# Query bias of a fused attention and mixture-of-experts layer carried by the query weights instead of by a matmul of its own

## The reference, cut to what matters

```python
xn = _layernorm(x)                                  # (x - mean) / sqrt(var + eps) over the 256 channels
q = (xn @ Wq + bq).reshape(b, h, t, dh)             # b=4, h=16, t=1024, dh=128
k = (xn @ Wk + bk).reshape(b, t, h, dh).transpose(0, 2, 3, 1)
v = (xn @ Wv + bv).reshape(b, t, h, dh).transpose(0, 2, 1, 3)
logits = einsum('bhtd,bhds->bhts', q, k) / sqrt(dh) # causal mask, softmax
out = einsum('bhts,bhsd->bhtd', softmax(logits + mask), v)
attn = out.transpose(0, 2, 1, 3).reshape(b, t, h * dh) @ Wo + bo
# moe: shared expert + top 6 of 64 experts, 128 slots each, on the same xn
x = x + attn + moe
```

## Time and profile before

| | |
|---|---|
| median of 3 runs | 1869.17 us (1868.74 to 1877.19) |
| the profiled execution | 1875.93 us |
| its span, first to last instruction | 1874.2 us, 49686 instructions |
| PE matmul busy | 1696.9 us (91%) |
| PE weight loads busy | 1312.7 us (70%) |
| DVE busy | 1402.9 us (75%) |
| ACT busy | 1081.9 us (58%) |
| POOL busy | 1116.8 us (60%) |
| bias matmuls L592 | 128, 49.7 us busy |
| granted PE clock, mean | 0.962 of full speed |

### The profile page before, as it was taken

How to read it: one execution, slowest core, us unless ns; L and a number is a source line. 1 busy time by engine, 2 the same in 40 slices (tenths; PEclk the granted TensorE clock), 3 DMA queues, 4 the chain that set the end, 5 groups by cost and what they waited for, 6 DMA issues and landing times. The chain is left out here.

```text
span 1874.2 us, 49686 instructions
## 1 busy us (share of the span) xinstructions
PE 1696.9 (91%) x19217; PEld 1312.7 (70%) x19217; DVE 1402.9 (75%) x3128; ACT 1081.9 (58%) x2347; POOL 1116.8 (60%) x1006
## 2 busy tenths in 40 slices
PE   3699999999999999999977789999998999999997
PEld 3477777776777777777756767777776777767775
DVE  8677777777677777777644458888888888888885
ACT  2566666666666666666622255665655655666554
POOL 1256666767767676676720047666666666666653
PEclk8799999999999999999977689999999999999998
DMA  9377767666656656557557657777778778877775
GB/s 372 104 152 130 128 108 133 125 121 109 115 87 101 102 98 95 100 97 125 99 120 217 181 103 137 124 128 127 151 131 143 126 144 133 134 125 125 151 119 110
DMA packets 686658, 245.04 MB, mean 131 GB/s; under 512 B 637456, under 2 KB 674721, under 8 KB 685536
## 3 DMA queue, kind: packets, MB, share of 16 engines
q1 hardware_dynamic: 657472, 197.83, 59.2%
q0 software_dynamic: 18432, 33.64, 7.1%
q10 hardware_dynamic: 10528, 10.49, 1.7%
HBM read 57.11 MB, written 50.46 MB: 57 GB/s over the span
## 5 line engine op out<-in xcount | busy, mean ns | idle before, releaser
L485 POOL TENSOR_TENSOR prob<-prob 128x128 f16<-128x128 f32 (+7 forms) x512 | 652.5, 1279 | 636.5 <-ACT prob L874 630.0
L867 ACT ACTIVATE prob<-prob,nmax 128x128 f32<-128x128 f32 (+7 forms) x512 | 396.8, 775 | 598.4 <-DVE prob L1312 552.3
L708 PE MATMUL ps_s<-kT,qT 128*128 128x512 f16 (+3 forms) x2304 | 460.0, 327 | 4.4 <-DVE prob L1312 4.3
L723 PE MATMUL ps_o<-probT,vh 128*128 128x256 f16 (+1 forms) x3840 | 427.4, 265 | 3.4 <-DMA probT<-prob 3.4
L1312 DVE TENSOR_SCALAR_CACHE_REDUCE prob<-ps_s,neg_scale 128x128 f32<-128x128 f32 (+7 forms) x512 | 412.1, 809 | 11.3 <-PE ps_s L710 7.4
L723 PEld LDWEIGHTS ps_o<-probT,vh 128*128 128x128 f16 x3840 | 368.3, 99 | 49.4 <-issue 5.2
L874 ACT CAST prob<-prob 128x128 f16<-128x128 f32 (+7 forms) x512 | 341.4, 667 | 2.6 <-DMA probT<-prob 0.3
L708 PEld LDWEIGHTS ps_s<-kT,qT 128*128 128x128 f16 x2304 | 201.5, 98 | 144.7 <-issue 4.5
L737 PE MATMUL ps_y<-wo,oT 128*128 128x256 f16 x1536 | 211.6, 274 | 58.1 <-DVE oT L1327 55.8
L1341 DVE SCALAR_TENSOR_TENSOR resid<-ps_y,yscale,resid 128x256 f32<-128x256 f32 x512 | 223.1, 477 | 15.0 <-PE ps_y L737 5.3
L525 POOL DMA_INDIRECT got<-expert_out,slot_idx x192 | 196.2, 1022 | 32.5 <-issue 28.5
(11 more groups left out here) (182 smaller groups left out, 1661.0 us busy)
## 6 DMA issues: line engine op xcount, KB each, us to landing
dispatched<-zeros SPq DMA_DIRECT2D x16, 512.0 KB, 14.3
probT<-prob SPq DMA_TRANSPOSE x512
ex<-dispatched SPq DMA_DIRECT2D x16, 512.0 KB, 4.5
expert_out<-eo ACTq DMA_DIRECT2D x16, 512.0 KB, 3.7
eup<-in_L_ffn_w_up_dram SPq DMA_DIRECT2D x64, 64.0 KB, 2.1
dispatched<-xn,slot_idx POOLq DMA_INDIRECT x192
xn_columns<-xnth SPq DMA_DIRECT2D x24, 128.0 KB
got<-expert_out,slot_idx POOLq DMA_INDIRECT x192
```

The costliest lines, as they stand in the source:

```text
L485: pool.tensor_tensor(low_cols(j), prob_cols(j).rearrange("p (r k) -> p r k", k=P), high_cols(j), ALU.subtract).then_inc(p_low, 1)
L708: pe.matmul(s_cols(j, lo, hi), qT[:, u, a, j * P:(j + 1) * P], kT[:, u, c, lo:hi], start=(n == 0), stop=(n == 2 and hi < w))
L723: mm = pe.matmul(ps_o[:, lo:2 * P], vh[:, u, a, r * D:(r + 1) * D], probT[:, PT_AT[c] + 2 * r + s, lo:], start=(r + n == 0), stop=(r == 2 ...
L867: nc.scalar.activation(prob_cols(j), prob_cols(j), ACT.Exp, bias=nmax[:, j:j + 1], scale=-1.0, accum_out=rsum[:, i % 2, j:j + 1]).then_inc ...
```

## The change

Since a normalised token sums to zero over its 256 channels, a constant row can be subtracted from all rows of `Wq` without changing the product. The change subtracts row 0 of `Wq` from every row, so that row 0 becomes zero and channel 0 of the tokens no longer counts; it then writes `bq` into row 0 and replaces channel 0 of the tokens by ones. The bias matmul goes. Because keys and values still need the true channel 0, the queries get a copy `xq` of the first 128 channels: partition 0 holds ones (high half) and zeros (low half), partitions 1 to 127 are copied from `xT` or from DRAM. The second 128 channels are still read from `xT`.

```diff
             sp.wait_ge(bias_zero, 1)
-            for n, b in enumerate((bq, bq, bk, bv)):
+            for n, b in ((0, bq), (2, bk), (3, bv)):
...
             for n in (0, 1, 3, 2):
                 sp.dma_start(stg[n].rearrange("p (k n) -> p k n", k=(KC, KC, KC, H)[n]), views[n]).then_inc(wload[n], 16)
+                if n == 0:
+                    sp.dma_start(wq_row0, Wq[0:1, :].rearrange("a n -> (a n)").partition_broadcast(P)).then_inc(row0_in, 16)
...
-            sp.dma_start(resid[:, TB:2 * TB, :], x_v[:, TB:2 * TB, :]).then_inc(x_in[1], 16)
             sp.wait_ge(xn0_ready, TB)
             sp.dma_start(xn_d, xn0[:]).then_inc(xn0_stored, 16)
+            sp.wait_ge(xt0_low, 4)
+            sp.dma_start(xq[1:P, :, :], xT[1:P, :, 0, :]).then_inc(xq_in, 16)
+            sp.wait_ge(wq_shifted, 1)
+            sp.dma_start(resid[:, TB:2 * TB, :], x_v[:, TB:2 * TB, :]).then_inc(x_in[1], 16)
             sp.wait_ge(const_ready, 1)
...
                 for n in range(2):
                     sp.dma_start(xT[:, n, :, 0:TPH], xnT_d[:, n, :, b * T:b * T + TPH]).then_inc(xT_head, 16)
+                sp.dma_start(xq[1:P, :, 0:TPH], xnT_d[1:P, :, 0, b * T:b * T + TPH]).then_inc(xT_head, 16)
                 for n in range(2):
                     sp.dma_start(xT[:, n, :, TPH:], xnT_d[:, n, :, b * T + TPH:(b + 1) * T]).then_inc(xT_in, 16)
+                sp.dma_start(xq[1:P, :, TPH:], xnT_d[1:P, :, 0, b * T + TPH:(b + 1) * T]).then_inc(xT_in, 16)
...
+            pool.memset(xq[0:1, 0, :], 1.0).then_inc(xq_ones, 1)
+            pool.memset(xq[0:1, 1, :], 0.0).then_inc(xq_ones, 1)
+            pool.wait_ge(wload[0], 16)
+            pool.wait_ge(row0_in, 16)
+            pool.wait_ge(wmax_step, 1)
+            w3 = stg[0].rearrange("p (k n) -> p k n", k=KC)
+            pool.tensor_tensor(w3, w3, wq_row0.unsqueeze(1).to_broadcast([P, KC, HD]), ALU.subtract).then_inc(wq_shifted, 1)
...
                 elif h == 0 and half == 0:
-                    pe.wait_ge(xT_head, 32 * (i // H))
+                    pe.wait_ge(xT_head, 48 * (i // H))
...
                 if i == 0 and half == 0:
-                    pe.wait_ge(bq_step, 3)
-                    pe.wait_ge(bias_taken, 2)
-                pe.matmul(ps_t[:, half, :].rearrange("p (m t) -> p m t", t=TPH), bq_rows[:],
-                          bq_pick[:, half * (H // 2):(half + 1) * (H // 2)].unsqueeze(2).to_broadcast([P, H // 2, TPH]),
-                          start=True, stop=False)
+                    pe.wait_ge(xq_in, 16)
+                    pe.wait_ge(xq_ones, 2)
...
-                                           xT[:, c, k, h * TPH:(h + 1) * TPH], start=False, stop=(n + k == 3 and m % (H // 2) == H // 2 - 1))
+                                           (xT[:, c, k] if k else xq[:, c])[:, h * TPH:(h + 1) * TPH], start=(n + k == 0), stop=(n + k == 3))
...
                 elif h == 0 and half == 0:
-                    pe.wait_ge(xT_in, 32 * (i // H))
+                    pe.wait_ge(xT_in, 48 * (i // H))
...
+            act.wait_ge(wq_shifted, 1)
+            act.dma_start(stg[0][0:1, 0:HD], bq.rearrange("(a n) -> a n", a=1)).then_inc(bq_in, 16)
             def high_weights(n):
                 act.wait_ge(wscale_step, 8 if n < 2 else 20)
+                if n == 0:
+                    act.wait_ge(bq_in, 16)
...
-                    dve.wait_ge(bq_step, 1)
-                    V.tensor_scalar(bq_rows[0:64, :], bias_rows[0:64, :], scales[0:64, 0:1], None, ALU.mult).then_inc(bq_step, 1)
-                    dve.wait_ge(bq_step, 2)
-                    V.scalar_tensor_tensor(bq_rows[32:64, :], bias_rows[32:64, :], scales[32:64, 0:1], bq_rows[32:64, :],
-                                           ALU.mult, ALU.subtract).then_inc(bq_step, 1)
...
-            V.tensor_tensor(bq_pick[:], ident[:, 0:H], ident[:, 32:32 + H], ALU.add).then_inc(bias_taken, 1)
```

More of the change, by code:

```diff
@@ L78, in causal_attention_with_moe @@
         bkT = sb("bkT", [P, H])
-        bq_rows = sb("bq_rows", [P, D], F16)
-        bq_pick = sb("bq_pick", [P, H], F16)
         scales = sb("scales", [P, 4])
@@ L148, in causal_attention_with_moe @@
         spare = sb("spare", [P, 1792])
+        xq = sb("xq", [P, 2, T], F16)
         ps_s = ctx.enter_context(nc.psum_tensor("ps_s", [P, 2, 2 * 512], F32))
@@ L212, in causal_attention_with_moe @@
         q_done = sem("q_done")
-        bq_step = sem("bq_step")
+        row0_in = sem("row0_in")
+        wq_shifted = sem("wq_shifted")
+        bq_in = sem("bq_in")
+        xq_ones = sem("xq_ones")
+        xq_in = sem("xq_in")
         q_high = sem("q_high")
@@ L276, in causal_attention_with_moe @@
         stg = [t[:] for t in stg] + [resid[:, 2 * TB:, :].rearrange("p t c -> p (t c)")]
+        wq_row0 = resid[:, TB:2 * TB, :].rearrange("p t c -> p (t c)")
         tmp = ExitStack()
@@ L455, in _ @@
             pool.memset(bias_rows[:], 0.0).then_inc(bias_zero, 1)
-            pool.memset(bq_rows[:], 0.0).then_inc(bq_step, 1)
             pool.memset(zeros[:], 0.0).then_inc(const_ready, 1)
@@ L556, in _ @@
             pe.wait_ge(const_ready, 5)
-            pe.wait_ge(bias_in, 64)
+            pe.wait_ge(bias_in, 48)
             pe.transpose(ps_o[:, 0:P], bias_rows[:], ident[:]).then_inc(bias_done, 1)
@@ L1175, in _ @@
             V.tensor_copy(bkT[:], ps_o[:, 64:64 + H]).then_inc(bias_taken, 1)
-            V.tensor_tensor(bq_pick[:], ident[:, 0:H], ident[:, 32:32 + H], ALU.add).then_inc(bias_taken, 1)
-            dve.wait_ge(bias_taken, 2)
+            dve.wait_ge(bias_taken, 1)
             V.tensor_reduce(biasmax[:, 0:1], ps_o[:, 0:H], AX.X, ALU.max, apply_absolute_value=True).then_inc(wmax_step, 1)
```

## The result

| | before | after |
|---|---|---|
| median | 1873.15 us (1868.74 to 1877.19) | 1936.27 us (1934.16 to 1939.78, 4 runs) |
| ratio of the times | | 1.033, 95% interval 1.0313 to 1.0348 |
| span of the profiled execution | 1874.2 us | 1934.1 us |
| granted PE clock, mean | 0.962 | 0.947 |

The median of before is taken over the runs that were made beside those of after; it is 4 us above the one that the prediction was made against. Against it the change costs 63.1 us; the prediction's sum was +62.5 us.

A forecast was written before the change was run, and what follows sets the result against it. The prediction took a chain between DVE and ACT, with PE nearly saturated, to bound the kernel. Bias matmuls -3, start +8.5, turns +54 and clock +3 made +62.5 us: 1932 us against the median, range 1905 to 1970 us.

The forecast's parts named there:

- The turns: At the three turns, keys wait for the tail of `xq` on one DMA engine: +54 us together.
- The clock's share: After 15 us of idling at a turn, PE is granted the lower clock for a while: +1 us per turn.
- The choice of 20 us for the tail: At the turns, the tail of `xq`, 487,680 bytes in 1920-byte pieces on one engine, was taken to need 20 us.
- rival C: At the turns, the tail runs at the mixed rate, 14 us more per turn: up to 1983 us; chance 0.08.
- The start: PE's first query product waits for the copy into `xq` on one engine: +8.5 us (7 to 12).
- I cost this at nothing: At the start, row 0 of `wq` being ready later adds nothing, hidden by PE's wait for `xq` until 55 us.
- The bias matmuls: In the query projection, removing 28.2 us of PE time wins only waits that PE ends: -3 us (0 to -8).
- the prediction is wrong [...] if the period of the steady heads changes: A sign against the forecast: in the steady heads, the period per head was to stay the same.
- the 0.2 to 0.4 us that I named: In heads 36 to 62, PE's waits for `oT` grow by this much, with the same 25.6 us per head.
- Rival A: At start and turns, the 127-row transfers spread over 16 engines: about 1866 us, 1880 us at most; chance 0.13.
- Rival B: Over the whole kernel, PE's occupancy is the limit, so all 28.2 us come off: 1841 us; chance 0.02.
- The low ends: Smallest values for tail, head piece, start, clock and bias matmuls, given as +42 us together, 1911 us.

The follow-up runs named there:

- e4: The change with its transfers at the turns cut into 122 and 5 partitions, the start as in the change: 1902.98 us, ratio 1.0156.
- e1: The change with each of its 127-partition transfers cut into 112 and 15 partitions, at the start and the turns: 1879.45 us, ratio 1.0026.
- e5: The kernel before without the bias matmul, its vector operations and waits kept, query bias missing from the result: 1875.04 us, ratio 1.0002.
- e8: The kernel before with its two query-bias tiles declared last, instructions the same: 1873.70 us, ratio 1.0000.
- e11: The change with 112 and 15 partitions, but without POOL's subtraction of row 0 of the weights: 1873.17 us, ratio 0.9993.
- e6: The kernel before with each bias matmul issued twice, result the same: 1885.87 us, ratio 1.0052.
- e3: The change with the tail of `xq` on its own semaphore, so that keys do not wait for it: 1933.99 us, ratio 1.0312.
- e7: The change with 112 and 15 partitions, plus one more all-reduce on POOL ahead of the subtraction: 1894.02 us, ratio 1.0103.
- e12: The kernel before without the bias matmul and without DVE's three bias instructions and their waits: 1874.05 us, ratio 1.0001.

## Why the prediction was right, step by step

**The turns, +54 us and +3 us for the clock: right, in size and cause.** The keys came 18.7, 17.6 and 17.5 us later behind their marks than in before; my steps gave 18.2, 18.1 and 17.7 us. With the heads behind them the turns cost 57.4 us, predicted 57. The queries started 4.6, 3.4 and 3.1 us late (predicted 3.4 us); at the first turn SP issued its first load 1.6 us later behind the mark than before, which I had not foreseen. The clock's share was close to my 1 us: in the 4 us behind the first turn's wait PE was granted 0.54 of full speed, then 1.00 again, and the first half of the keys took 2.74 us instead of the 1.46 us of the earlier trace rows. At the other two turns it was granted 0.50, the lower of its two levels, for as long. The choice of 20 us for the tail over the 33.9 us of rival C was right: 26.1 GB/s per engine, taken from the clearing of the slots, was measured as 25 GB/s in the copy and 26.7 GB/s between after and e4. Rival C would have given 1983 us.

**The start, +8.5 us: right.** Measured +8.9 us. The first query product came at 56.80 us instead of 55 us, since the copy took some 22 us from the landing of the store ahead of it, against 19.9 us by the bytes. The transposes came at 79.94 us (predicted 78.9 us). "I cost this at nothing, because PE waits for `xq` until 55 us and that wait hides it" held in the change. What the cover hides was mis-described: I had the subtraction and the load of `bq` in mind. What lay under it was the 5.8 us ahead of POOL's all-reduce. Once the transfers are spread it is no longer covered: 4.0 us at the first mark of e1.

**The bias matmuls, -3 us: wrong.** The step "What comes through is what PE ends today: 2.5 us in the first heads" counted the waits that PE ended as time to be won. e5 measured 0 (-1.5 to +2.2 us by its interval). In heads 1 to 14 ACT's wait for the query products went from 2.5 us to 0.6 us with the change, and these heads took 0.3 us less (1.4 us less in e5, but 0.8 us less in e8 too, which still has the matmul). The change did gain 2.7 us in its steady heads, most of it in heads 17 to 30 by a gap on DVE that I had not seen and that, by the prediction's own terms, counts against it: "the prediction is wrong [...] if the period of the steady heads changes". The number was right by chance. In heads 36 to 61 the forecast held: PE's waits for keys grew from 14.8 to 20.0 us and those for `oT` from 31.0 to 35.9 us, 10.1 us together, while 26 heads lost 11.4 us of matmuls, with the same 25.6 us per head. What was taken from PE came back as waits. For `oT` alone that is 0.19 us per head, just under the 0.2 to 0.4 us that I named. Timeline of PE in after, head 49, to be held against the earlier trace rows:

```profile
1534.90 0.20 PE L615 MATMUL ps_t<-xq,wq 128*128 128x64 f16 x1 [0.84 <-DVE kT L1314]
1538.20 0.83 PE L753 MATMUL ps_y<-wo,oT 128*128 128x256 f16 x6 [1.19 <-DVE oT L1342]
```

**Rival A, the transfers spread.** e1 is built to be that world: 1879.45 us, where the rival said about 1866 us and at most 1880 us. Set against the runs of before made beside it, e1 is 4.9 us slower (by the ratio) where the rival said 3 us faster. Of these 8 us the subtraction is 6.3 us by e11; the queries' waits at the turns, which I had put at +0.3 us each, grew by 5.2 us in all. Together that is more than 8 us, since the gain of the gap on DVE works against them and turns vary.

**Rival B, PE is the bound.** Refuted in the direction of this change by e5. e6 shows how near it was: 28 us more of PE's work cost 10 to 12 us.

**The range.** The low ends that the prediction lists for its range add up to +43.7 us and not to +42 us; nothing else hangs on this.

## What to carry to other kernels

Count the rows of a DMA's slowest dimension before its bytes: 127 partitions moved at 25 GB/s where 128 move at 417, and cutting the transfers into 112 and 15 brought back 57 of 63 us. Freeing the one consumer that waits was no cure while the transposes stood behind the slow transfer (e3). Relieving an engine that shows waits of its own gave nothing here (e5), and it may still be the next bound: remove a suspected cost and double it, since the two answers can differ (0 and some 11 us here).

## What the runs showed of the hardware that I had not expected

- On POOL a tensor operation and an all-reduce over partitions are not neighbours for free: 5.8 us from one to the other in e1, 9.9 to 11.1 us at each of three changes in e7. Why it was shorter in e1 is open; the two all-reduces in a row at the end of e7 show no such gap of their own, as the second waits for DVE. Whether the gap comes from the change of operation or from what the two MODIFY_POOL_CONFIG do was not tested.
- A gap of 0.26 us on DVE in each pair of heads between 590 and 870 us went with three DVE instructions far earlier in the program (e12 against e5); moving the tiles did not take it away (e8).
- SP can be held for long in the issue of a DMA behind one that goes to a single engine: 17 us for a transpose at the turn, and at the start the load of the second batch behind the copy, 0.5 us of issuing in e1, took 18.84 us in after (SP's timeline). The clearing DMAs were issued from 46.84 us on instead of 28.53 us:

```profile
27.95 18.84 SPq L367 DMA_DIRECT2D resid<-in_L_attn_x_dram  x1
```
